# Narrow attention of a one-core block: the rows of values made once per batch and put in place per head by one-hot products

## The reference

```python
def proj(x, W, b):
    y = jnp.einsum('bld,ed->ble', x, W) + b
    return y.reshape(x.shape[0], x.shape[1], H, HD).transpose(0, 2, 1, 3)
Q = proj(q, Wq, bq)      # q = layernorm(x), 2 x 1024 rows
K = proj(k, Wk, bk)      # k = v = context, 2 x 77 rows
V = proj(v, Wv, bv)
scores = jnp.einsum('bhqd,bhkd->bhqk', Q, K) * scale
scores = jnp.where(mask[:, None, None, :], -jnp.inf, scores)
attn = jax.nn.softmax(scores, axis=-1)
out = jnp.einsum('bhqk,bhkd->bhqd', attn, V)
out = out.transpose(0, 2, 1, 3).reshape(q.shape[0], q.shape[1], D)
return jnp.einsum('bld,ed->ble', out, Wo) + bo
```

## Time and profile before

| | |
|---|---|
| median of 3 runs | 1747.47 us (1746.74 to 1753.26) |
| profiled execution | 1749.65 us, its span 1747.8 us |
| TensorE matmul, weight load | 84%, 71% of the span busy |
| VectorE, ScalarE, GpSimd | 63%, 43%, 37% |
| mean granted clock of TensorE | 0.908 of full |
| first stage | 0 to about 142 us, its loop from 50 |
| last attention | 1508 to about 1656 us, its loop from 1556 |

### The profile page before, as it was taken

How to read it: one execution, slowest core, us unless ns; L and a number is a source line. 1 busy time by engine, 2 the same in 40 slices (tenths; PEclk the granted TensorE clock), 3 DMA queues, 4 the chain that set the end, 5 groups by cost and what they waited for, 6 DMA issues and landing times. The chain is left out here.

```text
span 1747.8 us, 25282 instructions
## 1 busy us (share of the span) xinstructions
PE 1461.9 (84%) x9442; PEld 1234.9 (71%) x9442; DVE 1106.4 (63%) x2427; ACT 747.3 (43%) x1285; POOL 641.1 (37%) x436
## 2 busy tenths in 40 slices
PE   7998859998868999994798997656999999599854
PEld 5786658887658999994577775425887888568722
DVE  6675767886546767772656454475676675467578
ACT  2454534443116667661435433102334443044465
POOL 1452125566013556542122222104556555235200
PEclk9898889999869999997799998677999999699978
DMA  5000000000345777754100000404444433500001
GB/s 182 1 1 5 1 1 1 1 1 1 111 149 181 216 216 228 221 160 82 59 1 1 1 1 1 134 4 155 85 98 93 99 85 49 114 1 1 1 0 49
DMA packets 94064, 122.02 MB, mean 70 GB/s; under 512 B 12188, under 2 KB 79159, under 8 KB 93943
## 3 DMA queue, kind: packets, MB, share of 16 engines
q1 hardware_dynamic: 72823, 91.56, 16.3%
q0 software_dynamic: 21120, 28.85, 9.1%
HBM read 94.95 MB, written 25.43 MB: 69 GB/s over the span
## 5 line engine op out<-in xcount | busy, mean ns | idle before, releaser
L2480 POOL DMA_INDIRECT ch_total<-ch_y,ch_index x64 | 107.4, 1678 | 123.8 <-DVE ch_y L2663 108.8
L1194 POOL DMA_INDIRECT t_total<-t_y,t_index x46 | 100.0, 2175 | 138.6 <-DVE t_y L1315 128.6
L3466 POOL TENSOR_TENSOR L_s<-L_s,L_mx 128x1232 f32<-128x1232 f32 x32 | 76.5, 2389 | 141.9 <-DVE L_mx L3545 141.9
L736 PE MATMUL t_ps<-t_hT_hi,t_w_hi 128*128 128x256 f32 x368 | 106.8, 290 | 7.6 <-DVE t_w_lo L1303 6.0
L736 PE MATMUL ch_ps<-ch_hT_hi,ch_w_hi 128*128 128x512 f32 x256 | 104.7, 409 | 9.7 <-DVE ch_hid L2689 6.3
L2600 ACT ACTIVATE ch_silu<-ch_ps 128x512 f32<-128x512 f32 x64 | 38.3, 599 | 172.8 <-PE ch_ps L738 170.7
L736 PE MATMUL t_ps<-t_w_hi,t_act_hi 128*128 128x256 f32 x368 | 105.8, 288 | 0.0
L737 PE MATMUL t_ps<-t_hT_lo,t_w_hi 128*128 128x256 f32 x368 | 105.6, 287 | 0.0
L738 PE MATMUL t_ps<-t_hT_hi,t_w_lo 128*128 128x256 f32 x368 | 105.6, 287 | 0.0
L738 PE MATMUL t_ps<-t_w_hi,t_act_lo 128*128 128x256 f32 x368 | 104.1, 283 | 0.0
L737 PE MATMUL t_ps<-t_w_lo,t_act_hi 128*128 128x256 f32 x368 | 104.1, 283 | 0.0
(11 more groups left out here) (518 smaller groups left out, 4447.6 us busy)
## 6 DMA issues: line engine op xcount, KB each, us to landing
t_w_in<-in_L_ffn_w1T SPq DMA_DIRECT2D x23, 1024.0 KB, 4.9
t_w_in<-in_L_ffn_w2T SPq DMA_DIRECT2D x23, 1024.0 KB, 5.6
ch_w_in<-in_L_ffn_w SPq DMA_DIRECT2D x24, 512.0 KB, 3.7
x<-in_x SPq DMA_DIRECT2D x4, 512.0 KB, 5.0
t_total<-x SPq DMA_DIRECT2D x1, 2048.0 KB
t_rows<-t2d_h SPq DMA_DIRECT2D x1, 2048.0 KB
x<-t_total SPq DMA_DIRECT2D x1, 2048.0 KB, 8.1
tb_w<-in_L_xattn_w SPq DMA_DIRECT2D x2, 1024.0 KB, 9.7
```

The costliest lines, as they stand in the source:

```text
L736: nc.tensor.matmul(out, sh, mh, start=start, stop=False)
L1194: nc.gpsimd.indirect_dma_start(out=total, out_offset=bass.IndirectOffsetOnAxis(ap=index[:, 2 * j + u:2 * j + u + 1], axis=0), in_=y[:, j % ...
L2480: nc.gpsimd.indirect_dma_start(out=total, out_offset=at(s, u), in_=y[:, s % 2, u, :], in_offset=None, compute_op=ALU.add).then_inc(added[s ...
L3466: nc.gpsimd.tensor_tensor(s[:, n % G], s[:, n % G], spread(mx[:, n % G, :], 2, [P, H, KEYS]), ALU.subtract).then_inc(shifted, 1)
```

## The change

`context`, the tripled copy of the context, goes. Instead `values()` multiplies each batch's 77 context columns (as stationary operand) with all 256 columns of `wv`, once, into PSUM bank 1: rows of values, 77 keys by 256. ScalarE copies them to `v_rows` (77 x 2 x 256). It also makes `periods`, the 77 x 77 identity three times in a row. `values_in_place(half)` multiplies, for five chunks each, the slice of `periods` from `f * 128 % 77` on (77 x 128, one 1 per column) with the chunk's 48 columns of `v_rows` of both batches, 96 columns: this copies row `key` of the values to each row of the chunk. `values_taken(half)` masks them as before, now by halves of the chunks, in 2 + 3 operations instead of 2 + 2. In the queues, `values()` follows the keys, half 0 follows `turn_rows(0)`, half 1 follows `queries(0)`, and nothing follows `turn_rows(1)`. The wait for the last queries moves from before the loop to before the first `attend`, which writes the bank that they lie in.

```diff
-        context, touched = sb("context", [P, KC, B, 3 * KEYS]), sb("touched", [P, 1])
+        periods, touched = sb("periods", [KEYS, 3, KEYS]), sb("touched", [P, 1])
+        v_rows = sb("v_rows", [KEYS, B, D])
...
-        VB_BANK = (1, 2)
-        VB_OPS = 2
+        V_BANK, VB_BANK = 1, 2
+        VB_OPS = 5
...
+        def placed(half):
+            return ps[:, VB_BANK + half, 0:HALF * B * 3 * hd].rearrange("p (f b e) -> p f b e", f=HALF, b=B)
...
-            def values(b, lo, hi):
-                pe.wait_ge(context_ready, KC)
-                for f in range(lo, hi):
+            def values():
+                for b in range(B):
+                    for kc in range(KC):
+                        ins = nc.tensor.matmul(ps[0:KEYS, V_BANK, b * D:(b + 1) * D], k.ctxT[:, kc, b * KEYS:(b + 1) * KEYS],
+                                               wv[:, kc, :], start=(kc == 0), stop=(kc == KC - 1))
+                ins.then_inc(v_psum, 1)
+
+            def values_in_place(half):
+                pe.wait_ge(periods_ready, 1)
+                pe.wait_ge(v_rows_ready, 1)
+                for f in range(half * HALF, (half + 1) * HALF):
                     rows, (h0, _) = rows_of(f), heads_of(f)
                     at, wide = f * P % KEYS, min(3, H - h0) * hd
-                    for kc in range(KC):
-                        ins = nc.tensor.matmul(ps[0:rows, VB_BANK[b], f * 3 * hd:f * 3 * hd + wide],
-                                               context[:, kc, b, at:at + rows], wv[:, kc, h0 * hd:h0 * hd + wide],
-                                               start=(kc == 0), stop=(kc == KC - 1))
+                    ins = nc.tensor.matmul(placed(half)[0:rows, f % HALF, :, 0:wide],
+                                           periods[:].rearrange("n r m -> n (r m)")[:, at:at + rows],
+                                           v_rows[:, :, h0 * hd:h0 * hd + wide], start=True, stop=True)
                 ins.then_inc(vb_psum, 1)
...
                 if n:
                     pe.wait_ge(o_ready, n)
+                else:
+                    pe.wait_ge(q_ready, NG * HC16)
...
             constants(pe)
             keys()
-            values(0, 0, HALF)
+            values()
             turn_rows(0)
-            values(0, HALF, FC)
+            values_in_place(0)
             queries(0)
-            values(1, 0, HALF)
+            values_in_place(1)
             turn_rows(1)
-            values(1, HALF, FC)
             pe.wait_ge(kbd_ready, 2 * HC16)
-            pe.wait_ge(vb_ready, 2 * VB_OPS)
+            pe.wait_ge(vb_ready, VB_OPS)
             scores(0)
...
-            pe.wait_ge(q_ready, NG * HC16)
...
-            for kc in range(KC):
-                nc.scalar.copy(context[:, kc].rearrange("p b (r n) -> p b r n", n=KEYS),
-                               spread(k.ctxT[:, kc, :].rearrange("p (b n) -> p b n", b=B), 2, [P, B, 3, KEYS])
-                               ).then_inc(context_ready, 1)
+            nc.scalar.copy(periods[:], spread(k.ident[0:KEYS, 0:KEYS], 1, [KEYS, 3, KEYS])).then_inc(periods_ready, 1)
+            act.wait_ge(v_psum, 1)
+            nc.scalar.copy(v_rows[:].rearrange("n b d -> n (b d)"), ps[0:KEYS, V_BANK, :]).then_inc(v_rows_ready, 1)
             act.wait_ge(q_loaded, 32)
...
-            def values_taken(b):
-                dve.wait_ge(vb_psum, 2 * (b + 1))
-                of = vb[:, b].rearrange("p f (h e) -> p f h e", e=HEAD)[:, :, :, 0:hd]
-                made = ps[:, VB_BANK[b], 0:FC * 3 * hd].rearrange("p (f h e) -> p f h e", f=FC, e=hd)
-                h_last = H - heads_of(FC - 1)[0]
-                nc.vector.tensor_tensor(of[:, 0:FC - 1], made[:, 0:FC - 1],
-                                        k.own_head[:, 0:FC - 1].unsqueeze(3).broadcast_to([P, FC - 1, 3, hd]), ALU.mult
-                                        ).then_inc(vb_ready, 1)
-                nc.vector.tensor_tensor(of[0:LAST, FC - 1, 0:h_last], made[0:LAST, FC - 1, 0:h_last],
-                                        spread(k.own_head[0:LAST, FC - 1, 0:h_last], 2, [LAST, h_last, hd]), ALU.mult
-                                        ).then_inc(vb_ready, 1)
+            def values_taken(half):
+                dve.wait_ge(vb_psum, half + 1)
+                fs = slice(half * HALF, min((half + 1) * HALF, FC - 1))
+                n = fs.stop - fs.start
+                for b in range(B):
+                    nc.vector.tensor_tensor(
+                        vb[:, b, fs].rearrange("p f (h e) -> p f h e", e=HEAD)[:, :, :, 0:hd],
+                        placed(half)[:, 0:n, b].rearrange("p f (h e) -> p f h e", e=hd),
+                        k.own_head[:, fs].unsqueeze(3).broadcast_to([P, n, 3, hd]), ALU.mult).then_inc(vb_ready, 1)
+                if half:
+                    h_last = H - heads_of(FC - 1)[0]
+                    nc.vector.tensor_tensor(
+                        vb[0:LAST, :, FC - 1].rearrange("p b (h e) -> p b h e", e=HEAD)[:, :, 0:h_last, 0:hd],
+                        placed(half)[0:LAST, HALF - 1].rearrange("p b (h e) -> p b h e", e=hd)[:, :, 0:h_last],
+                        k.own_head[0:LAST, FC - 1, 0:h_last].unsqueeze(1).unsqueeze(3).broadcast_to([LAST, B, h_last, hd]),
+                        ALU.mult).then_inc(vb_ready, 1)
```

More of the change, by code:

```diff
@@ L3187, in narrow_attention @@
         later_loaded = sem("later_loaded")
-        keys_psum, kbd_ready, context_ready = sem("keys_psum"), sem("kbd_ready"), sem("context_ready")
+        keys_psum, kbd_ready, periods_ready = sem("keys_psum"), sem("kbd_ready"), sem("periods_ready")
+        v_psum, v_rows_ready = sem("v_psum"), sem("v_rows_ready")
         table_ready, own_key_ready = sem("table_ready"), sem("own_key_ready")
```

## The result

The changed kernel takes 1739.51 us (median; 1732.31 to 1744.27) against 1748.15 for the kernel before (1746.74 to 1753.26, measured beside it): ratio 0.9941, 95% interval 0.9917 to 0.9964. Measured again beside the experiments, on two chips, it was 0.9963 (0.9943 to 0.9982) and 0.9950 (0.9931 to 0.9969). The forecast was 1739.7.

What follows compares the result with a forecast made beforehand. TensorE was taken to bound the run-ups, VectorE next by 6.56 and 6.05 us. The 12.4 us gained, less 2 x 2.3 for the low clock, left 7.8: from 1747.47 to 1739.7 us, range 1733.5 to 1744.5.

Steps and rivals of the forecast that it cites:

- VectorE as the next bound: Run-ups: VectorE's idle 6.56 and 6.05 us vanishes and VectorE just becomes the bound; gain 12.4 us together.
- S at 25.9 us: Start of the first scores in the first stage: forecast 25.9 us, where it was 32.41.
- The products: TensorE run-up: 256-column products 3.4 us for 4.19; one-hot halves 2.1 us for 3.95 and 1.4 for 2.5 + 2.15.
- The 77 rows of contraction: One-hot products on TensorE: contraction of 77 rows instead of 128; no row priced it, nothing taken off.
- The clock: TensorE's clock rises near the values' end, then falls after 3.5 us idle; scores and queries(1) run at 1.2 GHz.
- From S to A: From first scores to first attend, just ahead of the loop: low clock costs 2.3 us per stage, range 1.2 to 4.0.
- The moved wait: TensorE's 0.78 us stand before the first transposes of probabilities goes; gain between 0 and 0.8 us per stage, taken as 0.
- Sum: Both run-ups: 12.4 - 2 x 2.3 = 7.8 us gained.
- the first case: Low clock falls in both stages' run-ups: gain 5.5 to 9.5 us, loops' clock as noise; chance 0.45.
- rival (4): Low clock shifts inside the loops: 25 us more cancels the gain, 42 us more gives 1756; chance 0.04.

Runs made afterwards that it cites:

- e1_fill: Changed kernel plus three extra 512-column products in TensorE's idle time before the first scores, both stages; 0.9970 of the kernel before, 0.9966 when repeated.
- e8_order_on_before: Kernel before with all 80 records of values ahead of queries(0), taken by VectorE before the second statistics; 1754.30 us against 1747.25.
- e6_values_first_rows: Changed kernel with both value halves placed before queries(0), taken before the second statistics, and last rows normalised with the others; 1736.86 us, ratio 0.9938.

## Why the prediction was right

- **VectorE as the next bound, S at 25.9 us.** Measured 26.13, of which 0.25 us is a later start of the loads. The gain at S is 6.28 and 5.97 us, 12.25 in sum, forecast 12.4. VectorE's new operations took 24.00 - 23.36 = 0.64 us and 0.66 us (25.29 to 25.95), forecast 0.64 and 0.68.
- **The products.** 10 records of 96 columns took 1.33 and 1.16 us; the forecast for a half at the high clock was 1.1. The 77 rows of contraction gave nothing back and cost nothing. The products of 256 columns took 3.42 us in the last stage (forecast 3.4) and 2.48 in the first, because there the clock rose inside them.
- **The clock.** It rose during the values, and fell in the last microsecond of the idle time of 4.37 and 3.27 us (forecast 3.5) or within 0.4 us behind it, in both stages and in all three profiles of the changed kernel. From S to A 21.53 - 20.05 = 1.48 us and 22.71 - 20.05 = 2.66 us were added; without the moved wait's 0.17 it is 1.65 and 2.83, forecast 2.3 each, so the sum, 4.5 for 4.6, is nearer than either part. In the other two profiles it is 1.65 and 2.81, 1.64 and 1.48. It is on the path up to the loop, as e1_fill shows. The Trainium skill (TensorE: Matmul & The Clock Gate, § Why this matters for your kernels) says that idle time of TensorE between bursts of matmuls brings its lower clock back; the trace agrees here, with 4.37 and 3.27 us of idle time and queries(1) at 5.06 and 5.92 us where the full clock takes 3.70.
- **The moved wait.** Forecast 0, between 0 and 0.8 us; measured 0.17 a stage.
- **Sum.** 12.25 - 4.14 = 8.1 us at the loops' start, forecast 7.8; at the end 8.6, 5.5 and 9.1 us in three measurements. That the median, 1739.51, is 0.2 us from the forecast is luck: the kernel before beside it was 0.7 us slower than the median from which the forecast starts, and the gain itself differs by 3.6 us from one measurement to the next.
- **Where it was thin.** The loops' clock was put down as noise of about 2 us in the range of the first case. It is more: see below. Its stretch of the first loop also ended too early, at 142 us; the loop's last addition to x comes at 153.96, so 24 us of it lay at the low clock and not 17. The measured ratios lie on both sides of 0.5%, within each other's intervals, and rival (4) is real as a spread though not as a shift that any run shows.

## What to carry to other kernels

Before making the busiest engine's run-up shorter, read which engine is next and by how much, and change the order on that engine in the same step: here two lines of order were worth as much as the new products, and they lost time without them. Idle time that a change opens ahead of dense matmuls on TensorE can cost twice, once as waiting and once at the low clock, as it did in all six stages of the changed kernel that were profiled. Where a weight load sets the price, as for the 48 and 96 columns here, batching more columns under it is free, but it gains only while that engine is the bound.

## What the runs showed that was not expected

The loops differ from execution to execution by more than the change is worth. These are the first-stage loops of e8_order_on_before and e6_values_first_rows, with the same 758 matmul records (clock third from the end):

```profile
55.90:147.19 91.29, 85.40 (x758) 73.94 (x758) 66.47 (x99) 45.83 (x91) 43.60 (x26) 1.00 0.01 1
```

```profile
42.92:145.71 102.79, 97.11 (x758) 82.97 (x758) 65.99 (x97) 46.37 (x91) 43.62 (x26) 0.87 0.00 1
```

91.29 us at full clock, 102.79 at 0.87: 2 x 0.13 x 102.79 = 27 us at the low clock, and half of them, about 13 us, is a little more than the difference of 11.5. All 28 profiled loops lie between these two, and each is 89.3 to 91.3 us plus half its time at the low clock. TensorE is busy for over 93% of both loops. In the middle of the loops none of its idle times is over 0.4 us, and the clock falls there all the same; what brings it down there no run shows. In 35 executions of the kernel before (1737.75 to 1756.18 us) the mean granted clock goes with the time (correlation -0.85), 0.37 us for each us at the low clock. A change of 0.3% in this kernel is therefore better read at the start of the loops than from medians, with the 1 us in mind by which S moved between two profiles of the same run-up.

The second surprise is the instruction queue: the fill's twelve matmul and load instructions ahead of the last attention went with a packet of 0.02 MB on that queue beside the issue of its loads, and x landed 1.5 us later, in both runs that had them and in none of the other twelve profiles.
